# A two-layer decoder kernel: order of mask and scores, wider casts, low parts by a product with minus one, and a new order of turns

## The reference

```
x = x + L0_attn(norm(x))     16 heads of 32, causal: softmax(where(mask, -1e9, (q k^T) * 32**-0.5)) v, q/k/v/out with biases
x = x + L0_xattn(norm(x))    32 query heads of 16 on 8 heads of the context, no mask
x = x + L0_ffn(norm(x))      gate/up/down of 2048 with weights and activations quantised in blocks of 32
x = x + L1_attn(norm(x))     a scan over time: h = exp(d*A)*h + d*d, read out by C, times a gate
x = x + L1_xattn(norm(x))    16 heads of 32 on the context, causal, no biases
x = x + L1_ffn(norm(x))      a dense product and two of eight low-rank experts per token
```

## Time and profile before

| | us |
|---|---|
| median of 3 runs (lowest, highest) | 1713.17 (1711.69, 1718.19) |
| the profiled execution, its own time | 1709.06 |
| its span from the first to the last instruction | 1707.2 |
| PE busy (matmuls) | 1407.3 (82%) |
| DVE busy | 1372.5 (80%) |
| ACT busy | 1034.3 (61%) |
| POOL busy | 434.4 (25%) |
| chain that ended last, shares | DVE 34%, PE 33%, ACT 12%, issue 9%, SyncE's queue 5% |

### The profile page before, as it was taken

One profiled execution on the slowest core, in us unless ns is written; L12 is line 12 of the kernel. 1 busy time (PEld: TensorE's weight loads), 2 busy tenths in 40 slices (PEclk: granted clock), 3 DMA queues, 4 the chain that ended last, 5 costly groups with the idle time before them and its releaser, 6 DMA issues.

```text
span 1707.2 us, 30917 instructions
## 1 busy us (share of the span) xinstructions
PE 1407.3 (82%) x11862; PEld 726.6 (43%) x11920; DVE 1372.5 (80%) x2111; ACT 1034.3 (61%) x1862; POOL 434.4 (25%) x486
## 2 busy tenths in 40 slices
PE   2777878777989898888877867889998999998986
PEld 2344435243444453434333323435454555454542
DVE  6979989998689796895878799977697878877743
ACT  3333274462763755754576769885898796978431
POOL 2522042331240421321240230231131313031310
PEclk9888889799999998998999989879999998998998
DMA  6303221202002012002030003101010101101020
GB/s 230 97 27 86 51 69 50 58 14 43 27 14 70 2 41 43 26 8 51 21 122 26 2 25 111 36 10 41 26 42 26 41 32 36 37 18 41 14 51 25
DMA packets 92081, 76.37 MB, mean 45 GB/s; under 512 B 9377, under 2 KB 73889, under 8 KB 91425
## 3 DMA queue, kind: packets, MB, share of 16 engines
q1 hardware_dynamic: 91936, 74.40, 16.0%
HBM read 39.24 MB, written 9.44 MB: 29 GB/s over the span
## 4 chain that ended last, share of the span: by engine, by line
DVE 34%; PE 33%; ACT 12%; issue 9%; SPq 5%; POOL 3%; DMA 2%; ACTq 0%; DVEq 0%; POOLq 0%
PE bank L194 10%; DVE mix_NM L1035 6%; DVE ssm_HS L1495 4%; PE bank L1135 3%; SPq L704 3%; PE bank L503 2%; PE bank L948 2%; DVE ffn_m L1089 2%; POOL attn_P L687 2%; DVE ffn_Z L1099 2%; PE bank L511 2%; PE bank L491 2%; PE bank L933 2%; ACT ssm_DA L1443 2%; PE bank L463 1%
## 5 line engine op out<-in xcount | busy, mean ns | idle before, releaser
L1008 ACT ACTIVATE mix_P<-bank 128x512 f32<-128x512 f32 x256 | 141.8, 604 | 60.6 <-PE bank L933 59.6
L1035 DVE TENSOR_REDUCE mix_NM<-bank 128x2 f32<-128x512 f32 x256 | 163.7, 683 | 16.5 <-PE bank L908 16.5
L687 POOL TENSOR_SCALAR_AFFINE_SELECT cross_P<-cross_P 128x256 f32<-128x256 f32 x128 | 95.3, 754 | 301.8 <-ACT cross_P L595 301.7
L1495 DVE TENSOR_TENSOR_SCAN ssm_HS<-ssm_DA,ssm_DD 128x1024 f32<-128x1024 f32 x64 | 151.1, 2361 | 20.5 <-ACT ssm_DD L1446 14.7
L687 POOL TENSOR_SCALAR_AFFINE_SELECT attn_P<-attn_P 128x256 f32<-128x256 f32 x128 | 99.9, 791 | 248.1 <-ACT attn_P L595 247.8
L1253 POOL TENSOR_TENSOR ffn_room<-ffn_room 128x512 f32<-128x512 f32 x64 | 87.7, 1370 | 247.3 <-ACT ffn_room L1192 140.5
L1443 ACT ACTIVATE ssm_DA<-ssm_Z,A_T 128x255 f32<-128x255 f32 x256 | 111.7, 500 | 6.8 <-DVE ssm_HS L1495 6.5
L595 ACT ACTIVATE attn_P<-bank 128x384 f32<-128x384 f32 x128 | 63.6, 497 | 56.7 <-PE bank L492 55.9
L595 ACT ACTIVATE cross_P<-bank 128x384 f32<-128x384 f32 x128 | 62.8, 491 | 50.6 <-PE bank L492 50.2
L933 PE MATMUL bank<-mix_Q,mix_K 64*128 64x256 f16 x512 | 53.5, 288 | 37.5 <-DMA mix_Q<-mix_NQL 20.9
L1418 ACT ACTIVATE ssm_Z<-bank 128x512 f32<-128x512 f32 x128 | 72.2, 601 | 19.7 <-PE bank L1331 19.2
(11 more groups left out here) (404 smaller groups left out, 4092.0 us busy)
## 6 DMA issues: line engine op xcount, KB each, us to landing
attn_stack<-attn_P SPq DMA_DIRECT2D x64, 128.0 KB, 2.5
cross_stack<-cross_P SPq DMA_DIRECT2D x64, 128.0 KB, 2.5
ffn_room<-f_gate SPq DMA_DIRECT2D x4, 1024.0 KB, 5.9
XR<-x SPq DMA_DIRECT2D x8, 512.0 KB, 8.1
attn_stack<-attn_P SPq DMA_DIRECT2D x64, 64.0 KB, 2.2
ffn_room<-f_up SPq DMA_DIRECT2D x4, 1024.0 KB, 5.1
ffn_room<-f_down SPq DMA_DIRECT2D x4, 1024.0 KB, 4.8
x_mid<-XR SPq DMA_DIRECT2D x8, 512.0 KB, 3.1
```

The costliest lines, as they stand in the source:

```text
L687: nc.gpsimd.affine_select(out=diagonal, in_=diagonal, compare_op=ALU.is_ge, fill=0.0, base=0, pattern=[[0, 2], [1, P]], channel_multiplier ...
L1008: nc.scalar.activation(self.p[h % 8], bank[b4[h % 2]][:, :], ACT.Exp, scale=HD2 ** -0.5).then_inc(s["p_ready"], 1)
L1035: nc.vector.tensor_reduce(self.nm[:, t, 16 * i + 2 * g:16 * i + 2 * g + 2], bank[b4[u % 3]][:, :].rearrange("p (c k) -> p c k", c=2), AX.X ...
L1495: nc.vector.tensor_tensor_scan(flat(self.hs), flat(self.da), flat(self.dd), 0.0, ALU.mult, ALU.add).then_inc(s["hs_ready"], 1)
```

## The change

1. The low parts of the first attention's queries and keys. VectorE's two subtractions per block are gone. PE adds minus the high part into the bank that still holds the product, by one matmul of 512 columns with a new constant `negative` (minus the identity), and ScalarE writes the remainder plus the bias as the low part. On PE and ACT this is one more turn per block, two blocks behind the products; on DVE four turns per batch are gone. The bank stays taken until ScalarE is done.
2. The second attention casts both halves of a block in one instruction of 512 elements, and subtracts them in one.
3. For this the parts lie in the order high, low, high, low in memory. One transfer per group of heads that took two neighbours at once becomes two: 20 instead of 16 transfers in both attentions.
4. In every odd unit of scores the mask is added first, so that the masks of an even unit and of the next odd one can follow each other, as can the scores of an odd unit and of the next even one. From unit 5 on the scores of odd units are split in two matmuls of 128 columns.
5. The three loaders of weights share their semaphores one after another, and a loader waits at its start until the one before it has finished.
6. All five strings of `TURNS0` are new (they are left out below).

```diff
-        identh = sb(top, "identh", [P, P], F16)
+        identh, negative = sb(top, "identh", [P, P], F16), sb(top, "negative", [P, P], F16)
...
-        Q_LOW, K_HIGH, Q_HIGH, K_LOW = range(4)
+        Q_HIGH, Q_LOW, K_HIGH, K_LOW = range(4)
...
+                if i == 0 and self.before is not None:
+                    sp.wait_ge(*self.before.ready())
...
-                for c in range(DC):
+                for c in range(DC + 2):
+                    if c >= 2 and self.bq is not None:
+                        yield
+                        pe.wait_ge(self.qh_ready, DC * n + c - 1)
+                        nc.tensor.matmul(bank[self.b[c % 3]][:, :].rearrange("p (i k) -> p i k", i=2), negative[:],
+                                         self.qk[:, Q_HIGH:K_LOW:2, c - 2, :], start=False, stop=True,
+                                         skip_group_check=True).then_inc(self.ql_ps, 1)
+                    if c >= DC:
+                        continue
...
+                    masked = u % 2 == 1
+                    for part in ("mask", "scores") if masked else ("scores", "mask"):
...
+                                for keys in (slice(0, P), slice(P, S)) if masked else (slice(0, S),):
...
-                            pe.wait_ge(self.stack_in, 16 * 16 * (n + 1))
+                            pe.wait_ge(self.stack_in, 16 * 20 * (n + 1))
...
+                    if c >= 2 and self.bq is not None:
+                        yield
+                        act.wait_ge(self.ql_ps, DC * n + c - 1)
+                        for i, part, bias in ((0, Q_LOW, self.bq), (1, K_LOW, self.bk)):
+                            last = nc.scalar.activation(self.qk[:, part, c - 2, :], bank[self.b[c % 3]][:, i * S:(i + 1) * S],
+                                                        ACT.Identity, bias=bias[:, c - 2:c - 1])
+                        last.then_inc(self.qk_ready, 1)
...
+                    if self.bq is None:
+                        last = nc.scalar.copy(self.qk[:, Q_HIGH:K_LOW:2, c, :],
+                                              bank[self.b[(2 + c) % 3]][:, :].rearrange("p (i k) -> p i k", i=2))
...
-                for c in range(DC):
+                for c in range(DC if self.bq is None else 0):
...
+                    src = bank[self.b[(2 + c) % 3]][:, :].rearrange("p (i k) -> p i k", i=2)
+                    nc.vector.tensor_tensor(self.qk[:, Q_LOW:K_LOW + 1:2, c, :], src,
+                                            self.qk[:, Q_HIGH:K_LOW:2, c, :], ALU.subtract).then_inc(self.qk_ready, 1)
...
                                            (1, slice(0, 2), slice(Q_LOW, K_HIGH + 1)),
-                                           (2, slice(0, 2), slice(Q_HIGH, K_LOW + 1))):
+                                           (2, slice(0, 1), slice(Q_HIGH, Q_HIGH + 1)),
+                                           (2, slice(1, 2), slice(K_LOW, K_LOW + 1))):
```

More of the change, by code:

```diff
@@ L31 @@
[L31 to L35, removed]
@@ L215, in make_constants @@
             own(nc.gpsimd.memset(identh[:], 0.0))
+            own(nc.gpsimd.memset(negative[:], 0.0))
             own(nc.gpsimd.memset(hide_qk[:], 0.0))
@@ L227, in make_constants @@
                                             pattern=[[-1, P]], channel_multiplier=1))
+            own(nc.gpsimd.affine_select(out=negative[:], in_=negative[:], compare_op=ALU.not_equal, fill=-1.0, base=0,
+                                        pattern=[[-1, P]], channel_multiplier=1))
             own(nc.gpsimd.affine_select(out=hide_qk[:], in_=hide_qk[:], compare_op=ALU.is_ge, fill=MASKED,
@@ L243, in __init__ @@
                     self.loaded, self.high_ready, self.low_ready = before.loaded, before.high_ready, before.low_ready
-                self.first = 0 if before is None else len(before.items)
-                self.used = [0 if before is None else len(range(i, len(before.items), len(stage))) for i in range(len(stage))]
+                self.before = before
+                self.first = 0 if before is None else before.first + len(before.items)
+                self.used = [0 if before is None else before.used[i] + len(range(i, len(before.items), len(stage)))
+                             for i in range(len(stage))]
             def ready(self, count=None):
@@ L360, in __init__ @@
                 self.weights = weights
+                self.ql_ps = sem(f"{name}_ql_ps") if bq is not None else None
                 for_sems = lambda part: sem(f"{name}_{part}") if before is None else before.signals[part]
@@ L571, in act @@
                             act.wait_ge(small_in, 48)
[L572 to L577 removed]
+                    if self.bq is None:
+                        last = nc.scalar.copy(self.qk[:, Q_HIGH:K_LOW:2, c, :],
+                                              bank[self.b[(2 + c) % 3]][:, :].rearrange("p (i k) -> p i k", i=2))
+                    else:
+                        for i, part, bias in ((0, Q_HIGH, self.bq), (1, K_HIGH, self.bk)):
+                            last = nc.scalar.activation(self.qk[:, part, c, :], bank[self.b[(2 + c) % 3]][:, i * S:(i + 1) * S],
+                                                        ACT.Identity, bias=bias[:, c:c + 1])
                     last.then_inc(self.qh_ready, 1)
@@ L1777, in build @@
                 (whole(xkv_w), M["xkv"].rearrange("p (a n) -> p a n", a=2))],
-                [z[:, 8 * i:8 * i + 8, :].rearrange("p h t -> p (h t)") for i in range(3)])
+                [z[:, 8 * i:8 * i + 8, :].rearrange("p h t -> p (h t)") for i in range(3)], weights_0)
             weights_f = Loader("l1f", [
```

175 lines of the change are left out of this document (85 added, 90 removed).

## The result

The changed kernel takes 1723.16 us, median of 10 runs (1717.74 to 1729.38), against 1713.97 (1709.83 to 1718.19) for the kernel before on the same chip; the ratio is 1.0057 with a 95% interval of 1.0042 to 1.0073. It is slower by 9.8 us; the forecast was 1696, with 1680 to 1715 as the range. The profiled execution took 1729.17 us, its span is 1727.0.

What follows compares the result with a forecast made beforehand. No engine bounds the whole: VectorE is fullest from 100 to 400 us, shares with TensorE to 990, and TensorE leads from 1200 to 1600. Terms -9 +2 -1 -4 -1 +4 -6 -2 = -17 took 1713.2 to 1696 us, range 1680 to 1715.

Steps and rivals of the forecast that it cites:

- Four more transfers per batch: SyncE's queue: four more issues hold it 2.7 us longer per batch; +4 us taken, ends +2.7 and +22.
- Turns moved: SyncE: mixer's row maxima issued ahead of the stack shorten TensorE's waits; -6 us taken, ends 0 and -13.
- the last sign of being wrong: Would show the forecast wrong: moved turns make an engine wait in its written order for late work; no size.
- Low parts and joined casts: First attention's low parts off VectorE: -9, ScalarE handover +2; second attention's joined casts and subtractions: -1 us.
- the products' 6.8 us: TensorE, first attention: 32 added negative products of 512 columns at 0.21 us each, 6.8 us in all.
- Rival (d): Negative products wait on TensorE for ScalarE's casts and stall the queues: 1734 us at 1.2 us each; chance 0.10.
- Rival (b): All of each saving reaches the end, on VectorE, the queue and the second layer: about -31, 1682 us; chance 0.14.
- Masks: Score units, masks first by turns: fewer shape changes on TensorE; -1 us in the first layer, -4 in the second.
- 0.11 us per change of shape: TensorE: each change from one stationary shape to another costs 0.11 us; 89 and 103 fewer changes counted.
- rival (e): Shape change is not what the 0.11 us is, so two masks in a row save nothing: 1702 us; chance 0.06.
- The start: Kernel start: three 0.5 MB loads no longer all stand ahead of the weights; -2 us, ends +3 and -5.
- The prediction's 0.2 us for four issues: SyncE: four issues at the skill's 50 ns dispatch; the prediction set it aside for 2.7 us from the queue rows.

Runs made afterwards that it cites:

- 1: Changed kernel with 16 instead of 20 stack transfers per batch, second attention's low parts again in two subtractions: 1692.43 us, ratio 0.9861 to the kernel before.
- 3: Kernel before with 20 instead of 16 stack transfers per batch, same bytes, nothing else changed: 1740.82 us, ratio 1.0142.
- 9: Changed kernel with 16 stack transfers per batch and SyncE's order of turns of the kernel before: 1679.91 us, ratio 0.9808 to the kernel before.
- 2: Changed kernel, still 20 transfers, with only SyncE's order of turns put back to that before: 1712.53 us, ratio 0.9981 to the kernel before.
- 6: Kernel before, its own order of turns and 16 transfers, with new low parts, joined casts, shared loaders and masks first by turns: 1703.66 us, ratio 0.9941.
- 13: Changed kernel with 16 transfers and SyncE's old turns, plus five one-column Softplus instructions that bring ten table loads back: 1686.78 us, ratio 0.9827 to the kernel before.
- 14: Changed kernel with 16 transfers and SyncE's old turns, plus five one-column Exp instructions that load no table: 1676.16 us, ratio 0.9769 to the kernel before.
- 5: Kernel before, its own order of turns and 16 transfers, with new low parts, joined casts and shared loaders, no masks first: 1708.42 us, ratio 0.9969.
- 4: Kernel before with only the masks first in odd units, keys split in two matmuls from unit 5 on: 1702.68 us, ratio 0.9927.

## Why the prediction was wrong, point by point

**The step that failed is "Four more transfers per batch".** The queue time of 2.7 us a batch was right (2.6), and the upper end, +22, was named; I took +4 because "in the seven batches before it the order of turns has two to nine units of other work to put under the wait". The runs give +33.6 in the new order and +24.3 in the old (1 and 3), 2.1 and 1.5 us in each of 16 batches, and +29.6 in the new order with SyncE's old turns (9 to 2). The end +22 itself was too low, since it charged eight of the sixteen batches; the other eight, the first layer's, pay too, behind or ahead of the mixer's small transfers. The term also left out TensorE's clock behind each stand, by the estimate in experiment 1 up to 16 us of the 33.6. Why the counted units of work were no cover is my reading and not shown: that work was already standing under the ten microseconds that sixteen issues take.

**"Turns moved", SyncE: sign wrong.** -6 was taken; the moved turns cost 9.1 us with sixteen transfers (uncertain by 7) and 13.1 with twenty (9 and 2 against 1 and the changed kernel). The mixer's waits fell as foreseen, 20.9 to 10.9. What got no price is what is queued behind the waiting instruction, although the last sign of being wrong names it ("moved turns that make an engine wait in its written order for work that is late"). A stack that is ready now stands up to 19.3 us behind the moved turns; in the batch shown above 15.1 us of that is SyncE's wait for VectorE (308.09 to 323.16), and the rest the issues ahead of the stack.

**Turns moved on the other engines: not in the sum at all.** From 6 to 9 only the turns of the compute engines change, at sixteen transfers and SyncE's old order: -22.8 us (uncertain by 6), 1079 to 1085 in the first part and 618 to 598 in the rest. I gave them nothing. The ten table loads saved are a likely part of it, some 10 us by 13 against 14, but 13 put ten loads back in places of its own and lost only 3 to 7 us against 9, so the share is not pinned down. The loads could have been counted: the groups of the kernel before show 69 of 1283 ns, and the order of Softplus and Exp turns follows from TURNS0. They also explain most of what ScalarE shows: its busy time rose by 21 us in 5, and only by 3.7 in the changed kernel, which has 12.8 us fewer loads. What earns the rest stays open. The traces have one more difference, that from 1200 to 1600 us the clock is 0.94 in 6 and 0.98 in 9; no run tells whether that is a cause or follows from fewer stands.

**Low parts and joined casts: about right alone, but not as a term to be added.** -9 and +2, a third of the products' 6.8 us where no masks pay for it, and -1 for the casts are -6; 5 measured -5.3 (-8.6 to -2.1). On top of the masks the same edit gave +2.4 (4 to 6), so in a sum that holds both it is nearer to nothing. Rival (d) is refuted: 2.5 us of waiting in 32 products, 0.08 each, where it began to matter at 0.5. (The reading of the earlier trace rows under (d) is slightly off: of the 62.8 us that the casts waited, TensorE had 56.5 and VectorE 6.2.) Rival (b), all of it arrives, is refuted too.

**Masks.** The 0.11 us per change of shape is confirmed. TensorE's timeline in the changed kernel:

```profile
316.04 0.39 PE L481 MATMUL bank<-attn_P 32*128 32x128 f16 x4
316.37 0.60 PE L473 MATMUL bank<-hide_qk,ident 128*128 128x512 bf16 x2
316.91 0.39 PE L481 MATMUL bank<-attn_P 32*128 32x128 f16 x4
```

Two masks in a row hold it 0.54 us, where two apart take 2 x 0.32, so rival (e) is refuted too. (Beside it the prediction takes the 0.33 us of four L908 matmuls with the step for half of what four in a row would take; four in a row with the step would be 0.53, and half holds only less the step, 0.22 against 0.42.) What a pair saves is small beside VectorE's pace in the same stretch,

```profile
312.34 5.10 DVE L1062 TENSOR_REDUCE mix_NM<-bank 128x2 f32<-128x512 f32 x8 [0.23 <-PE bank L935]
```

0.64 us for each maximum. In the new order the saving ends there, or so I read it (+2 to +5 us in three runs). Why the old order gave 12.5 us without the low parts and 4.8 with them isn't shown; that both free the same time is the rival that fits, but no run here says which time.

**The sum.** By ratios: low parts and casts -5.3, masks -4.8, turns of the compute engines -22.8, turns of SyncE +9.1, four transfers +33.6, together +9.8. They close because each step starts from the last (5, 6, 9, 1, changed); in another order the single terms would differ, as masks and low parts show. Without the +4 for the four transfers the forecast would have been 1692, and run 1 measured 1692.4. That is luck in part: the -22.8 that I had left out made up for SyncE's turns, +9.1 in place of -6. The start, -2 in the sum, gave nothing that shows: the first stacked scores begin at 70.75, before at 69.11.

## What to carry to other kernels

Price an issue on a DMA queue like an instruction on an engine: 0.6 to 0.7 us of that queue, on the path wherever something already waits behind the queue's block. How much of it reaches the end belongs to the order of turns (9 to 34 of some 42 us here), and a matmul engine that has stood may work on at the lower clock level; the place to look is the idle time before the first reader, and one run with a few issues more, on the kernel before, tells it in advance. Before a small urgent transfer is moved ahead of a long block, compare when each becomes ready: an in-order queue that waits for the later one delays the one that is ready, and here the block first was worth 9 to 13 us. And where a change rewrites the order of one engine's work, count what that order itself costs, on ScalarE the changes of function table (1.0 us of time each in one pair of runs here, uncertain by 0.6), before calling it worth nothing.

## What the hardware showed that I had not expected

The time from issue to landing hardly matters here: the page gives 2.1 us for a 64 KB transfer,

```profile
attn_stack<-attn_P SPq DMA_DIRECT2D x128, 64.0 KB, 2.1
```

and that is paid once a block, behind the last issue that the scores need. Above that is the second row of maxima:

```profile
341.69 0.59 SPq L737 DMA_DIRECT2D attn_stack<-attn_NQL  x1
```

TensorE starts at 343.75, 2.06 us after this issue began. The Trainium skill ("DMA: Bandwidth & Descriptors", Anatomy of one DMA) gives a fixed cost of some 2 us for one transfer on GpSimd's path; on SyncE's this trace has nearly the same. For what comes before the data move, its table has about 50 ns of sequencer dispatch and, without a figure, "small, variable" for generating the descriptors. The prediction's 0.2 us for four issues took the first alone, and from GpSimd's path. Here one issue holds SyncE's queue 602 ns, median of 160:

```profile
L731 SPq DMA_DIRECT2D attn_stack<-attn_P x160: 587/602/1465, 49.4 to 820.5; - x160
```

A table load lasts 1.28 us, and the next instruction starts at once. ScalarE's timeline in 9:

```profile
1241.10 0.64 ACT L1445 ACTIVATE ssm_Z<-bank 128x512 f32<-128x512 f32 x1
1241.76 1.28 ACT L1470 ACT_TABLE_LOAD   x1
1243.05 1.70 ACT L1470 ACTIVATE ssm_DA<-ssm_Z,A_T 128x255 f32<-128x255 f32 x4
```

The Trainium skill ("ScalarE: Activation LUTs", What ACT_TABLE_LOAD costs) has the same 1283 ns, and adds a drain of 1380 ns for each change of set, 2.66 us in all. An estimate from that page's figure would be 27 us for ten loads. The trace shows no such gap here, 0.02 us before the load and 0.01 behind it, and the ten cost 10 us of the kernel's time (13 against 14).

The last surprise is how the price of an issue bends: in the order before, four a batch are worth 9 us below sixteen and 24 above; in the new order 26 and 34. The granted clock from 1200 to 1600 us bends with it: 0.94, 0.95 and 0.93 with twelve, sixteen and twenty transfers in the order before, and 1.00, 0.98 and 0.94 in the new one. Which follows from which no run here shows.
